# Value and output weights of a gated cross-attention layer multiplied in three rounded products

## The chip, the cores and the metric

The kernel runs on one core of one Trainium2 chip. The metric is the device time of one execution in microseconds (us). Three executions of the kernel before took 627.66, 628.72 and 630.34 us, the median being 628.72 us.

## The reference

A layer takes 1024 tokens of width 256 (16 sequences of 64) and a context of the same length and width 128. Cross-attention comes first, then self-attention and a mixture of experts:

```
q = rmsnorm(layernorm(x) @ Wq), k = rmsnorm(ctx @ Wk), v = ctx @ Wv      # 16 heads of 128
out = softmax(q k^T * scale) @ v ;  x = x + tanh(g_xattn) * (out @ Wo)
x = x + tanh(g_ffn) * (causal self-attention + experts of layernorm(x))
```

The kernel never forms v of the cross-attention. For each head it multiplies the value weights (128 x 128) by the output weights (128 x 256) once, `vo = Wv_h @ Wo_h`, and applies vo to the context rows that attention has averaged.

## The kernel before, in words

All work is written out by hand in one program per engine, in the fixed order in which each engine runs it, with semaphores between them. Stage a is the cross-attention, stage b the self-attention, stage m the experts. Each stage runs over two halves of 512 tokens. Stages a and b run over 8 pairs of heads per half, stage m over 25 chunks of hidden units.

Nearly every large product is made of "rounded products". An operand is rounded to float32r (`hi`), the rest is taken by subtraction (`lo`), and hi*hi + hi*lo + lo*hi replace one float32 product. VectorE makes most `hi` halves of weights by a copy (split_queries, L1491; split_values, L1517), ScalarE some of them, and GpSimd all `lo` halves through its helper `rest` (L1720).

The product vo is the exception. In the first half of stage a (`weighs_values`, 8 pairs), value_out (L692 to L699) multiplies the raw float32 weights of the two heads, `raw_a2`, straight into `bank_k`, 128 x 256 for each head. ScalarE rounds that result into `vo_hi` (take_value_out, L1117) and VectorE takes the rest `vo_lo` (split_value_out, L1526), which is the last thing in its body for a pair. The other pieces of the order that matter here:

- TensorE, pair u (cross_pair, L846): norm_q and scores of u, then context_values of the pair before (which writes bank_k among others and so waits for vo_lo of that pair), keys and queries of the next pair, the two outputs of the pair before, between them the second queries, and then value_out(u) and norm_k of the next pair (L718). project_keys for the next pair's first head waits for the semaphore `raw`: the VectorE product L1432 has read bank_s.
- VectorE, pair u (cross_pair, L1588): sums of squares (L1405 to L1409), scaling of the scores (L1432, L1437), maximum, lows of the context values (L1393), subtraction of the maximum (L1455), take_q (L1479), then in some pairs one piece in slot 2 of the preparation of the next tokens, then normalise (L1461 to L1465), the transposition L1473, the two copies L1491, and L1529. Pairs are counted from 0 here. Slot 2 holds the statistics of the second half's tokens (L1303 to L1309) in pair 3 and their mean subtraction `hn` (L1317, four instructions) in pair 4. Pair 5 turns the tokens.
- GpSimd, pair u (cross_pair, L1764): `wq_lo` and `wk_lo` of the two heads of the pair after the next (four subtractions), each after its `hi`. In pair 0 it also subtracts the second half of the context (`ctxt_lo`).
- SyncE: the weights raw_a2 of pair n are loaded again after value_out of pair n-1 (`vo_done`), and behind that in the same queue come the loads of the query and key weights of pair n+2.

Of the kernel before, what the change touches and what calls it, by code (L numbers as in the profile page):

```python
# [27 lines left out]
F32R = mybir.dt.float32r  # L28
# [4 lines left out]
P = 128  # L33
# [160 lines left out]
def flamingo_layer(nc, x, ctx_t, ctx, head_a, head_b, pair_v, chunk_m, small, out, shared_units):  # L194
    TOK, D = x.shape
    H = head_a.shape[0]
    C = ctx_t.shape[0]
# [19 lines left out]
    AQ, AK, AV, AO = 0, D, 0, C  # L217
# [14 lines left out]
    with ExitStack() as stack:  # L232
        def sb(name, shape, dt=F32):
            return stack.enter_context(nc.sbuf_tensor(name, shape, dt))
# [25 lines left out]

        raw_a = sb("raw_a", [P, 2 * A1])
        raw_a1 = [raw_a[:, p * A1:(p + 1) * A1] for p in range(2)]
        raw_a2 = [sb(f"raw_a2_{p}", [P, A2]) for p in range(2)]
        raw_b1 = [sb(f"raw_b1_{p}", [P, B1]) for p in range(2)]
        raw_b2 = [sb(f"raw_b2_{p}", [P, B2]) for p in range(2)]
        raw_m1 = [sb(f"raw_m1_{p}", [P, M1]) for p in range(2)]
# [64 lines left out]
        def stage_sems(tag, names):  # L331
# [1 line left out]
            return {n: sem(f"{tag}_{n}") for n in names.split()}  # L333

        A = stage_sems("a", "wq_hi wq_lo wk_hi wk_lo q_done k_done sq_q sq_k qt kt scores raw scaled max "
                       "sub exp sum inv norm attn_t vo_done vo_hi vo_lo ssk_done ssq_done ssq ln_q qt_1 "
                       "ln_k r_k r_q pv_done pv_hi pv_lo wo_done")

        B = stage_sems("b", "wq_hi wq_lo wk_hi wk_lo wv_hi wv_lo wo_hi wo_lo q_done k_done v_done qt kt vs scores scaled "
# [90 lines left out]
        def _(sp):  # L430
# [2 lines left out]
                sp.dma_start(raw_a1[h], head_a[2 * u.i + h, :, 0:A1]).then_inc(ld_a1[h], 16)  # L433

            def load_a2(u, h):
                sp.dma_start(raw_a2[h][:], head_a[2 * u.i + h, :, A1:A1 + A2]).then_inc(ld_a2[h], 16)

            def load_b1(u, h):
                sp.dma_start(raw_b1[h][:], head_b[2 * u.i + h, :, 0:B1]).then_inc(ld_b1[h], 16)
# [50 lines left out]
                load_m2(Unit(plan, "m", 0, h))  # L490
            for n in range(1, HALVES * PAIRS):
                if n < PAIRS:
                    sp.wait_ge(A["vo_done"], n)
                    for h in range(2):
                        load_a2(numbered("a", n), h)
                if n + 2 < HALVES * PAIRS:
                    reload_a1(n + 2)
# [58 lines left out]
        def _(pe):  # L556
# [135 lines left out]
            def value_out(u):  # L692

                pe.wait_ge(A["kt"], u.of(1) + 2)
                for h in range(2):
                    pe.wait_ge(ld_a2[h], 16 * u.n)
                    last = nc.tensor.matmul(bank_k[:, h * D:(h + 1) * D], raw_a2[h][:, AV:AV + C], raw_a2[h][:, AO:AO + D],  # L697
                                            start=True, stop=True)
                last.then_inc(A["vo_done"], 1)  # L699

            def norm_q(u):
# [568 lines left out]
        def _(v):  # L1270
# [248 lines left out]
            def split_out(u, h):  # L1519
# [3 lines left out]
                v.wait_ge(ld_b2[h], 16 * u.n)  # L1523
                nc.vector.tensor_copy(wo_hi[h][:], raw_b2[h][:]).then_inc(B["wo_hi"], 1)

            def split_value_out(u):  # L1526
                v.wait_ge(A["vo_hi"], u.n)
                two = slice(2 * u.i, 2 * u.i + 2)
                nc.vector.tensor_tensor(vo_lo[:, two, :], bank_k[:].rearrange("p (h n) -> p h n", h=2), vo_hi[:, two, :],  # L1529
                                        ALU.subtract).then_inc(A["vo_lo"], 1)  # L1530
# [57 lines left out]
            def cross_pair(u):  # L1588

                prev, nxt = u.prev(), u.next()  # L1590
                after = nxt.next()
                add_variance(u)
                scale_scores(u)
                hurried = prev and prev.very_first
                if hurried:
                    split_context_values(prev)
                take_max(u)
                if prev and not hurried:
                    split_context_values(prev)
                subtract_max(u)  # L1600
                if nxt.kind == "b":
                    split_values(nxt)
                    take_q(nxt, 0)
                if nxt.kind == "a":
                    take_q(nxt, 0)
                prepare_piece(*piece_at(u, 2), u)
                normalise(u)
                turn_weights(u)
                split_queries(after, 0, nxt)
                if after.kind == "b":  # L1610
                    split_keys(after, 0, nxt)
                prepare_piece(*piece_at(u), u)
                if nxt.kind == "b":
                    take_q(nxt, 1)
                split_queries(after, 1, nxt)
                if u.first and prev:
                    read_acc(prev)
                if not u.deferred:
                    split_context_values(u)
                if after.kind == "b":  # L1620
                    split_keys(after, 1, nxt)
                if u.weighs_values:
                    split_value_out(u)
# [93 lines left out]
        def _(pool):  # L1717
            def rest(lo, raw, hi, signal):

                nc.gpsimd.tensor_tensor(lo, raw, hi, ALU.subtract).then_inc(signal, 1)  # L1720
# [35 lines left out]
            def split_values(u):  # L1756
                pool.wait_ge(B["wv_hi"], u.n)
                rest(wv_lo[:], raw_v[:], wv_hi[:], B["wv_lo"])
# [5 lines left out]
            def cross_pair(u):  # L1764
                nxt = u.next()
                after = nxt.next()
                if nxt.kind == "b":
                    split_values(nxt)
                for h in range(2):
                    split_head(after, h)  # L1770
                if u.very_first:
                    pool.wait_ge(ctxt_hi_ready, HALVES)
                    rest(ctxt_lo[:, HT:TOK], ctxt[:, HT:TOK], ctxt_hi[:, HT:TOK], ctxt_lo_ready)
# [109 lines left out]
```

## Time and profile before

| what | value |
|---|---|
| median of 3 runs | 628.72 us |
| profiled execution, its own time | 627.96 us |
| span of the profiled execution | 626.1 us |
| TensorE matmuls | 617.8 us busy, 99% |
| VectorE | 461.7 us busy, 74% |
| ScalarE | 320.2 us busy, 51% |
| GpSimd | 254.0 us busy, 41% |
| mean granted TensorE clock | 1.00 |

The span runs from the first to the last instruction. A busy share is the time in which at least one instruction of an engine is under way; consecutive matmuls overlap in the record, so the distance from one start to the next is what one costs. In a row of the timeline the first number is the start in us and the second the length; "x4" means that four instructions are merged in it; the bracket tells how long the engine had been idle and what released it.

### The profile page before, as it was taken

To read this page: it belongs to the slowest core of one execution; us is meant where nothing else is said; L and a number is where in the kernel's file an instruction comes from. 1 tells how busy PE (TensorE), PEld (TensorE's weight loads), DVE (VectorE), ACT (ScalarE), POOL (GpSimd) and SP (SyncE) were. 2 spreads that over 40 slices of the span, in tenths; PEclk is the share of its full clock that TensorE was granted. 3 is DMA by queue.
4 is the path that set the end of the run, shared out by engine and by line. 5 is a ranking of instruction groups with operands and counts; after the bars stand their busy time and mean duration, and the time that the engine had idled before them with its cause. 6 is when DMAs were issued, how large, how long until landed. Compare 5 with 4: busy or idle time off the path is not lost.

```text
span 626.1 us, 17387 instructions
## 1 busy us (share of the span) xinstructions
PE 617.8 (99%) x6906; PEld 526.1 (84%) x6906; DVE 461.7 (74%) x934; ACT 320.2 (51%) x699; POOL 254.0 (41%) x336
## 2 busy tenths in 40 slices
PE   8999999999999999999999999999999999999997
PEld 6788888888889888999999889988878788888885
DVE  5979787997886886786677899567566976575554
ACT  6867677777743334243434333454476444444442
POOL 3221211313144334344343354345545665455552
PEclk9999999999999999999999999999999999999999
DMA  7532130111021322222231321123344333334442
GB/s 232 189 89 67 52 103 28 41 39 37 18 70 48 106 69 69 70 68 78 66 115 40 115 70 36 35 64 96 95 99 109 81 102 101 89 95 104 104 119 81
DMA packets 45757, 51.42 MB, mean 82 GB/s; under 512 B 12784, under 2 KB 32752, under 8 KB 45680
## 3 DMA queue, kind: packets, MB, share of 16 engines
q1 hardware_dynamic: 44976, 49.86, 27.8%
q8 instruction: 55, 0.90, 0.6%
q10 hardware_dynamic: 704, 0.48, 0.2%
q14 instruction: 22, 0.18, 0.1%
HBM read 48.22 MB, written 1.05 MB: 79 GB/s over the span
## 4 chain that ended last, share of the span: by engine, by line
PE 93%; ACT 3%; DVE 2%; issue 1%; DMA 1%; SPq 0%; DVEq 0%; ACTq 0%
PE bank_q L564 16%; PE acc L591 14%; PE bank_k L564 14%; PE acc L626 10%; PE bank_v L564 8%; PE bank_s L564 7%; PE bank_v L687 7%; PE bank_k L767 2%; PE bank_s L735 2%; PE bank_p L784 2%; PE bank_s L745 2%; PE bank_p L718 1%; PE bank_t L752 1%; PE bank_q L708 1%; PE bank_k L697 1%
## 5 line engine op out<-in xcount | busy, mean ns | idle before, releaser
L1720 POOL TENSOR_TENSOR wq_lo<-raw_a,wq_hi 128x256 fp32r<-128x256 f32 x32 | 23.5, 735 | 115.8 <-DVE wq_hi L1491 115.8
L1720 POOL TENSOR_TENSOR wq_lo<-raw_m,wq_hi 128x256 fp32r<-128x256 f32 x50 | 42.0, 840 | 60.9 <-DVE wq_hi L1510 59.5
L1554 DVE TENSOR_TENSOR pv_lo<-raw_a,pv_hi 128x512 fp32r<-128x512 f32 (+1 forms) x51 | 38.3, 753 | 30.8 <-ACT pv_hi L1135 30.2
L1135 ACT ACTIVATE pv_hi<-raw_a 128x512 fp32r<-128x512 f32 (+1 forms) x51 | 31.7, 623 | 55.4 <-DVE raw_a L1549 53.8
L564 PE MATMUL bank_q<-xt_hi,wq_hi 128*128 128x512 f32 x144 | 59.8, 416 | 0.0
L564 PE MATMUL bank_q<-xt_hi,wq_lo 128*128 128x512 f32 x144 | 56.8, 394 | 0.0
L564 PE MATMUL bank_q<-xt_lo,wq_hi 128*128 128x512 f32 x144 | 56.5, 393 | 0.0
L1541 DVE TENSOR_TENSOR r_k<-ln_k,unit_w 128x512 f32<-128x512 f32 x44 | 30.6, 696 | 32.1 <-ACT ln_k L1126 31.9
L1720 POOL TENSOR_TENSOR wk_lo<-raw_m,wk_hi 128x256 fp32r<-128x256 f32 x50 | 37.6, 753 | 30.5 <-ACT wk_hi L1210 30.5
L1720 POOL TENSOR_TENSOR wv_lo<-raw_v,wv_hi 128x512 fp32r<-128x512 f32 x16 | 20.7, 1294 | 67.9 <-DVE wv_hi L1517 67.9
L1720 POOL TENSOR_TENSOR wo_lo<-raw_m,wo_hi 128x256 fp32r<-128x256 f32 x50 | 41.5, 830 | 7.2 <-ACT wo_hi L1204 7.2
L1720 POOL TENSOR_TENSOR wq_lo<-raw_b,wq_hi 128x256 fp32r<-128x256 f32 x32 | 24.7, 772 | 48.5 <-DVE wq_hi L1494 48.5
L1057 ACT ACTIVATE kt<-bank_k 128x512 f32<-128x512 f32 x46 | 27.5, 599 | 32.2 <-PE bank_k L564 31.0
L564 PE MATMUL bank_k<-xt_hi,wk_lo 128*128 128x512 f32 x110 | 43.3, 394 | 0.0
L564 PE MATMUL bank_k<-xt_hi,wk_hi 128*128 128x512 f32 x110 | 43.2, 393 | 0.0
L564 PE MATMUL bank_k<-xt_lo,wk_hi 128*128 128x512 f32 x110 | 43.1, 392 | 0.0
L1069 ACT ACTIVATE vs<-bank_v 128x512 f32<-128x512 f32 x32 | 19.1, 598 | 44.6 <-PE bank_v L687 44.6
L626 PE MATMUL acc<-pv_hi,wo_hi 128*128 128x512 f32 (+1 forms) x102 | 40.6, 398 | 0.8 <-DVE pv_lo L1554 0.6
L626 PE MATMUL acc<-pv_hi,wo_lo 128*128 128x512 f32 (+1 forms) x102 | 40.1, 393 | 0.0
L626 PE MATMUL acc<-pv_lo,wo_hi 128*128 128x512 f32 (+1 forms) x102 | 39.9, 392 | 0.0
L591 PE MATMUL acc<-wo_hi,pv_hi 128*128 128x256 f32 x128 | 36.4, 284 | 0.0
L591 PE MATMUL acc<-wo_lo,pv_hi 128*128 128x256 f32 x128 | 36.2, 283 | 0.0
(254 smaller groups left out, 2097.3 us busy)
## 6 DMA issues: line engine op xcount, KB each, us to landing
raw_m<-in_chunk_m SPq DMA_DIRECT2D x50, 256.0 KB, 2.8
raw_a<-in_head_a SPq DMA_DIRECT2D x48, 192.0 KB, 3.1
raw_b<-in_head_b SPq DMA_DIRECT2D x32, 256.0 KB, 3.1
raw_m<-in_chunk_m SPq DMA_DIRECT2D x50, 128.0 KB, 2.1
raw_v<-in_pair_v SPq DMA_DIRECT2D x16, 256.0 KB, 2.9
raw_b<-in_head_b SPq DMA_DIRECT2D x32, 128.0 KB, 2.1
vs<-qt SPq DMA_DIRECT2D x32, 32.0 KB, 2.0
xs<-in_x SPq DMA_DIRECT2D x6, 128.0 KB, 3.3
```

The lines of the kernel that those rows point to most:

```text
L564: last = nc.tensor.matmul(bank[:], w[:, cols], m(k), start=n == 0, stop=n == 3 * chunks - 1)
L591: last = nc.tensor.matmul(acc[t // 2][:, (t % 2) * D:(t % 2 + 1) * D], w[:, tok], m, start=begins and n == 0, stop=True, skip_group_check= ...
L626: last = nc.tensor.matmul(acc[k][:, part], w[:, cols], m[:, part], start=u.first and n == 0, stop=True, skip_group_check=True)
L687: last = nc.tensor.matmul(bank_v[:, b * PAIR:(b + 1) * PAIR], m, w[:, cols], start=n == 0, stop=n == 3 * KD - 1)
L735: last = nc.tensor.matmul(bank_s[j * GROUP:(j + 1) * GROUP, g * SEQ:(g + 1) * SEQ], qt[:, h, queries], kt[:, h, at:at + SEQ], start=True, ...
L745: last = nc.tensor.matmul(bank_s[j * GROUP:(j + 1) * GROUP, g * SEQ:g * SEQ + seen], qt[:, h, queries], kt[:, h, at:at + seen], start=True ...
L1057: nc.scalar.activation(kt[:, h], bank[:], ACT.Copy).then_inc(stage["kt"], 1)
L1069: nc.scalar.activation(vs[u.n % 2][:, at:at + NT // 2, :], bank_v[:].rearrange("p (t n) -> p t n", n=PAIR), ACT.Copy).then_inc(B["vs"], 1)
L1135: nc.scalar.activation(pv_hi[:, u.parity, part], hh[:, part], ACT.Copy).then_inc(M["hh_hi"], 1)
L1541: nc.vector.tensor_tensor(gu, gs, weights, ALU.mult).then_inc(M["weighted"], 1)
L1554: nc.vector.tensor_tensor(pv_lo[:, u.parity, part], hh[:, part], pv_hi[:, u.parity, part], ALU.subtract)\
L1720: nc.gpsimd.tensor_tensor(lo, raw, hi, ALU.subtract).then_inc(signal, 1)
```

## The change

raw_a2 becomes one tensor for both heads of a pair (128 x 2 x 384). VectorE copies it, rounded, into `vo_in_hi` in one instruction after take_q and ahead of the piece in slot 2. GpSimd subtracts, in one instruction, into `vo_in_lo`, ahead of its four subtractions of the pair. value_out waits for vo_in_lo and issues three rounded products for each head in place of one float32 product. The load of the next raw_a2 waits for vo_in_lo in place of vo_done.

```diff
-        raw_a2 = [sb(f"raw_a2_{p}", [P, A2]) for p in range(2)]
+        raw_a2 = sb("raw_a2", [P, 2, A2])
+        vo_in_hi, vo_in_lo = sb("vo_in_hi", [P, 2, A2], F32R), sb("vo_in_lo", [P, 2, A2], F32R)
...
-                sp.dma_start(raw_a2[h][:], head_a[2 * u.i + h, :, A1:A1 + A2]).then_inc(ld_a2[h], 16)
+                sp.dma_start(raw_a2[:, h], head_a[2 * u.i + h, :, A1:A1 + A2]).then_inc(ld_a2[h], 16)
...
-                    sp.wait_ge(A["vo_done"], n)
+                    sp.wait_ge(A["vo_in_lo"], n)
...
                 pe.wait_ge(A["kt"], u.of(1) + 2)
+                pe.wait_ge(A["vo_in_lo"], u.n)
                 for h in range(2):
-                    pe.wait_ge(ld_a2[h], 16 * u.n)
-                    last = nc.tensor.matmul(bank_k[:, h * D:(h + 1) * D], raw_a2[h][:, AV:AV + C], raw_a2[h][:, AO:AO + D],
-                                            start=True, stop=True)
+                    for n, (w, m) in enumerate(((vo_in_hi, vo_in_hi), (vo_in_hi, vo_in_lo), (vo_in_lo, vo_in_hi))):
+                        last = nc.tensor.matmul(bank_k[:, h * D:(h + 1) * D], w[:, h, AV:AV + C], m[:, h, AO:AO + D],
+                                                start=n == 0, stop=n == 2)
...
+            def round_value_out(u):
+                for h in range(2):
+                    v.wait_ge(ld_a2[h], 16 * u.n)
+                if u.n > 1:
+                    v.wait_ge(A["vo_done"], u.n - 1)
+                nc.vector.tensor_copy(vo_in_hi[:], raw_a2[:]).then_inc(A["vo_in_hi"], 1)
...
                 if nxt.kind == "a":
                     take_q(nxt, 0)
+                if u.weighs_values:
+                    round_value_out(u)
                 prepare_piece(*piece_at(u, 2), u)
...
                     split_values(nxt)
+                if u.weighs_values:
+                    pool.wait_ge(A["vo_in_hi"], u.n)
+                    rest(vo_in_lo[:], raw_a2[:], vo_in_hi[:], A["vo_in_lo"])
                 for h in range(2):
                     split_head(after, h)
```

## Rows read from the trace of the kernel before

**Rows 1.** The page: busy time of TensorE, its granted clock in 40 slices, chain by engine

```profile
PE 617.8 (99%) x6906; PEld 526.1 (84%) x6906; DVE 461.7 (74%) x934; ACT 320.2 (51%) x699; POOL 254.0 (41%) x336
...
PEclk9999999999999999999999999999999999999999
...
PE 93%; ACT 3%; DVE 2%; issue 1%; DMA 1%; SPq 0%; DVEq 0%; ACTq 0%
```

**Rows 2.** Waits of TensorE in and after pair 0: us in total, times, longest

```profile
...
PE bank_p L718 <- ACT qt L1052: 0.8, 1, 0.8
...
```

**Rows 3.** The chain that ended last, pair 2: start, us, what

```profile
41.34 1.44 PE acc L591 x12
42.78 0.86 PE bank_k L697 x4
```

**Rows 4.** Timeline of VectorE, pair 2, with its start and end

```profile
38.64 0.68 DVE L1479 TENSOR_TENSOR qt<-bank_q,gqk 128x512 f32<-128x512 f32 x1
...
39.70 0.69 DVE L1461 TENSOR_REDUCE ex_sum<-ex 128x8 f32<-128x512 f32 x1 [0.38 <-ACT ex L1093]
...
40.66 0.69 DVE L1465 TENSOR_TENSOR attn<-ex,ex_inv 128x512 f32<-128x512 f32 x1
...
44.31 0.69 DVE L1529 TENSOR_TENSOR vo_lo<-bank_k,vo_hi 128x512 fp32r<-128x512 f32 x1 [1.76 <-ACT vo_hi L1119]
```

**Rows 5.** Groups by form: copies on VectorE, subtractions on GpSimd, 0 to 420 us

```profile
L1491 DVE CAST wq_hi<-raw_a 128x256 fp32r<-128x256 f32 x12 | 2.8, 267 | 0.0
...
L1517 DVE CAST wv_hi<-raw_v 128x512 fp32r<-128x512 f32 x16 | 6.7, 418 | 0.3 <-DMA raw_v<-in_pair_v 0.3
...
L1720 POOL TENSOR_TENSOR wq_lo<-raw_a,wq_hi 128x256 fp32r<-128x256 f32 x20 | 14.7, 737 | 66.3 <-DVE wq_hi L1491 66.3
```

**Rows 6.** Timelines of GpSimd and VectorE in a pair of stage b

```profile
206.75 1.29 POOL L1720 TENSOR_TENSOR wv_lo<-raw_v,wv_hi 128x512 fp32r<-128x512 f32 x1 [4.25 <-DVE wv_hi L1517]
...
207.53 1.05 DVE L1465 TENSOR_TENSOR attn<-ex,ex_inv 128x512 f32<-128x512 f32 x1
```

**Rows 7.** Timelines of VectorE and GpSimd at the start, 6.8 to 8.9 us

```profile
6.84 0.61 DVE L1317 TENSOR_SCALAR hn<-xs,mv 128x256 f32<-128x256 f32 x1
...
6.84 0.46 POOL L1720 TENSOR_TENSOR wk_lo<-raw_a,wk_hi 128x128 fp32r<-128x128 f32 x1 [5.38 <-ACT wk_hi L1234]
```

**Rows 8.** Timelines of VectorE and TensorE, pair 0

```profile
18.35 0.69 DVE L1479 TENSOR_TENSOR qt<-bank_q,gqk 128x512 f32<-128x512 f32 x1
...
19.56 1.02 PE L697 MATMUL bank_k<-raw_a 128*128 128x256 f32 x4
21.43 0.64 PE L718 MATMUL bank_p<-sq_k,ones_of 128*32 128x256 f32 x8 [0.84 <-ACT qt L1052]
```

**Rows 9.** Timelines of VectorE, GpSimd and the chain, pair 3

```profile
55.37 0.69 DVE L1529 TENSOR_TENSOR vo_lo<-bank_k,vo_hi 128x512 fp32r<-128x512 f32 x1 [0.29 <-ACT vo_hi L1119]
...
56.75 0.68 DVE L1432 TENSOR_TENSOR sc_sub<-bank_s,r_k 128x512 f32<-128x512 f32 x1
...
56.46 0.37 DVE L1409 TENSOR_TENSOR ssq<-sums_t,eps_q 128x8 f32<-128x8 f32 x1
...
56.08 0.73 POOL L1720 TENSOR_TENSOR wq_lo<-raw_a,wq_hi 128x256 fp32r<-128x256 f32 x1
...
57.70 0.90 PE bank_s L564 x3
```

**Rows 10.** Timeline of VectorE and the chain, pair 4

```profile
61.39 1.14 DVE L1317 TENSOR_SCALAR hn<-xs,mv 128x256 f32<-128x256 f32 x4
62.44 0.68 DVE L1461 TENSOR_REDUCE ex_sum<-ex 128x8 f32<-128x512 f32 x1
...
66.44 0.69 DVE L1529 TENSOR_TENSOR vo_lo<-bank_k,vo_hi 128x512 fp32r<-128x512 f32 x1 [1.17 <-ACT vo_hi L1119]
...
67.81 0.69 DVE L1432 TENSOR_TENSOR sc_sub<-bank_s,r_k 128x512 f32<-128x512 f32 x1
...
68.77 0.90 PE bank_s L564 x3
```

More of the change, by code:

```diff
@@ L335, in flamingo_layer @@
         A = stage_sems("a", "wq_hi wq_lo wk_hi wk_lo q_done k_done sq_q sq_k qt kt scores raw scaled max "
-                       "sub exp sum inv norm attn_t vo_done vo_hi vo_lo ssk_done ssq_done ssq ln_q qt_1 "
+                       "sub exp sum inv norm attn_t vo_in_hi vo_in_lo vo_done vo_hi vo_lo ssk_done ssq_done ssq ln_q qt_1 "
                        "ln_k r_k r_q pv_done pv_hi pv_lo wo_done")
```

## The prediction, made before the changed kernel had run

> **What bounds the kernel now.** I read the page first: matmuls are under way for 617.8 us of a span of 626.1, the chain that ended last is TensorE for 93%, and the granted clock is full, 2.4 GHz, in all 40 slices [rows 1]. So time is what TensorE issues plus what makes it wait. Next the waits of TensorE over the stretch that the change touches, the first half of stage a: from pair 0 on there is one, of 0.8 us, at norm_k in pair 0 [rows 2]. In pairs 1 to 7 TensorE runs without a gap, one pair every 11.07 us (the same step at 57.70 and 68.77 [rows 9, 10]), and every other engine has slack behind it. A saving on TensorE comes through in full there, and so does any new wait. The question is therefore what the products save, and whether the new VectorE copy and GpSimd subtraction use up the slack. All times below are read against the profiled execution, 627.96 us; it lies 0.76 below the median of 628.72.
>
> **The products.** In the chain, value_out of a pair takes 0.86 us (four records, two for each float32 product), and the twelve rounded products of the same 128x128 by 128x256 shape ahead of it take 1.44, 0.12 each [rows 3]. Six of them cost 0.72. The saving is 0.14 us a pair, where nothing else is late; over eight pairs at most 1.1 us. Bounds: nothing saved (0.86 again, should the six not follow each other so closely), or 0.2 a pair.
>
> **The copy on VectorE.** 128x768 has no row. 128x256 takes 0.27 and 128x512 0.42 [rows 5], so 0.15 for each 256, and 0.57 for 768; the low end is 0.5, the high end three separate 128x256, 0.8. I take 0.58.
>
> **The subtraction on GpSimd.** 128x256 takes 0.74 [rows 5], 128x512 1.29 [rows 6]: 0.55 for each 256, 1.85 for 768. Ends: 1.7, and 2.2 for three of 0.74.
>
> **What the long subtraction does to VectorE.** This is the larger cost. In stage b a GpSimd subtraction runs from 206.75 to 208.04; the VectorE product attn (ex times ex_inv, both in SBUF) begins at 207.53 and takes 1.05 us [rows 6] where it takes 0.69 otherwise [rows 4]. It ends 0.54 after the subtraction does, so it stood until GpSimd was through. The Trainium skill states it (SBUF — State Buffer, "Who interferes with whom"): an instruction of VectorE with two SBUF inputs, or a copy or scalar operation in its two-port mode, and one of GpSimd exclude each other for the whole instruction; tensor_reduce never contends. By that page and by these rows the sum is the same, but it speaks against this change, so it is worked through pair by pair.
>
> **Pairs 1, 2, 5, 6, 7.** Pair 2 stands for them [rows 4]. take_q begins at 38.64 and the next instruction can begin 0.6 later: copy 39.24 to 39.82. The sum over ex, which waits for ScalarE until about 39.7 anyway, shifts by 0.1. GpSimd, which has been idle for microseconds, subtracts from 39.9 to 41.75. attn wants to begin at 40.8, ends at 42.3 instead of 41.35: VectorE is now 0.95 late. It stays late until vo_lo, before which it had 1.76 us of idle time [rows 4]. So 0.8 is left, and the pair's end is as before. TensorE wants vo_in_lo as the second output ends, by the chain at 42.78 [rows 3], and has it at 41.8. No wait, 0.14 gained: 5 x 0.14 = 0.7 us. In pair 5 the cover is thinner, as two subtractions for the turned tokens lie behind attn.
>
> **Pair 0.** Here take_q begins at 18.35 [rows 8]: copy 18.95 to 19.53, GpSimd 19.6 to 21.45. TensorE, with no outputs to do, wanted to begin value_out at 19.56 and now begins at 21.5. It ends at 22.2, and norm_k begins then instead of 21.43 [rows 8]; the old 0.8 us wait there, for ScalarE's qt, hides the rest. ScalarE's vo_hi and what follows it (a context split, ln_k) move by 0.9 too, level with TensorE. Cost 0.8 us, bounds 0.6 and 1.2 (with the ends of copy and subtraction).
>
> **Pair 3.** Only 0.29 us of idle time lie before vo_lo, as the statistics fill VectorE [rows 9]. Copy 0.58 and a bit for the lock make it 0.6 late there, 0.3 after the idle time. The next thing that TensorE waits for is sc_sub, which ended at 57.43 with TensorE there by the chain at 57.70 [rows 9]: a slack of 0.27 at most; I use 0.2. So TensorE is 0.1 late, its 0.14 included. But ssq, two inputs, already stood behind a GpSimd subtraction here (0.37 us; the one from 56.08 to 56.81 [rows 9]), and with everything shifted it can meet the next one from its start: 0.4 more. I take 0.3; bounds 0.1 and 0.6.
>
> **Pair 4.** The four hn follow the copy at once, and they contend with GpSimd: at the start one of them took 0.61 where four in a row take 1.14 [rows 10], while GpSimd's subtraction, begun within the series, took its usual 0.46 [rows 7]. So a waiting GpSimd instruction gets in between two hn, and the next hn stands until it is through. Here: copy to 61.97, first hn, GpSimd from 62.2 to 64.05, then three hn, and the sum over ex begins at 64.8, not 62.44: 2.4 late [rows 10]. 1.17 of that goes into the idle time before vo_lo, 0.2 into the slack between sc_sub's end (68.50) and TensorE (68.77) [rows 10]. 1.0 us comes through, 1.5 if ssq stands behind a GpSimd subtraction again. I take 1.2. If all four hn went first, it would be 0.
>
> **Loads.** The next raw_a2 is asked for up to 0.8 us earlier than before, and is needed some 3 us earlier, at the copy; a period is 11 us, so at nothing. In pair 0 it is asked for 0.9 later, with 6 us to go. The four GpSimd subtractions and the reloads behind them in the SyncE queue move by 1 us within the same 11 us: nothing.
>
> **Sum.** 0.8 + 0.3 + 1.2 - 0.7 = +1.6 us (bounds of the parts: 0 to +2.9): 629.6 for an execution like the profiled one, 630.3 as a median. What TensorE loses in stage a it doesn't regain, for it has no gap later.
>
> **The rivals.**
> - *Only the saving shows* (the four hn go first, ssq slips by): pair 3 and pair 4 at zero, five or six pairs gain 0.14, pair 0 costs 0.8 or less. -0.1 to -0.5, 628.4. For it: the long idle times of VectorE before vo_lo [rows 4, 10]. Against: rows 7. Chance 0.2.
> - *No cheaper products*: the six rounded products take as long as the float32 ones, and the change doesn't do what it says. The 0.7 falls away: +2.3, 631.0. Rows 3 speak against it. Chance 0.08.
> - *Slower by over 0.5%*: GpSimd's 768 columns in one instruction take more than the row's slope gives. Place: each pair's attn and vo_in_lo. The point from which it decides: 2.6 us in place of 1.85; then attn eats the last 0.8 of VectorE's idle time in the plain pairs, and vo_in_lo comes after TensorE wants it. At 3 us each of the seven later pairs loses 0.4 to 0.5 and pairs 0 and 4 another 1.2 each: 1.6 + 0.7 + 3.2 + 2.4, about +7, 635.6; at 2.6 about +4, 632.7. For it: a subtraction of 128x256 and one of 128x512 are all there is. Against: their durations hardly vary. Chance 0.12.
>
> **How the numbers follow.** The forecast has the remaining 0.6. The likeliest time is 630.3. The range goes from 627.8, for the second case and an execution at the lower end of the runs shown, to 632.6, where the last case begins; a tenth is left out above, less than that below. About 0.5%, 3.1 us, is what a measurement of this kernel can tell from no change. Faster by that much would need three times the whole saving: 0.02. Slower by that much is the last case and the upper corner of the forecast: 0.13. The same: 0.85.
>
> **What would show it.** In the chain, value_out at 0.72 us for six products. On VectorE, one copy of 128x768 at 0.58; on GpSimd, one subtraction at 1.85; attn at 1.5 to 1.7 us in the plain pairs. TensorE's waits: pair 0, value_out for vo_in_lo, 1.9 us, with the 0.8 at norm_k gone; pair 4, about 1 us, at the context values for vo_lo or at project_keys for sc_sub; pair 3, a few tenths. An idle time before vo_lo of 0.8 us left in the plain pairs. I am wrong if TensorE waits in a plain pair, if one hn of pair 4 isn't lengthened by some 1.8 us, or if value_out takes as long as before.

## The result, and the profile after

| | before | after |
|---|---|---|
| median (9 executions each, same chip) | 628.77 us | 632.36 us |
| lowest to highest | 627.66 to 630.34 | 630.48 to 633.77 |
| profiled execution, its own time | 627.96 us | 633.46 us |
| span | 626.1 us | 631.7 us |

The ratio is 1.0055, with an interval of 1.0044 to 1.0065: the change costs 3.6 us. The predicted range (627.8 to 632.6) holds that, the predicted 630.3 does not reach it, and 0.55% is just past the 0.5% that separated "the same" from "slower". So the sign was right and the size was less than half of what came. The sections below say where the other 2 us are. The executions of one kernel spread over 2 to 3 us, and the profiled ones are single executions: that of the kernel before lies 0.8 us under its median, that of the changed kernel 1.1 us above.

The page of the changed kernel; [rows 1] answer to its first, third and last line:

```profile
PE 619.3 (98%) x6922; PEld 528.5 (84%) x6922; DVE 474.1 (75%) x942; ACT 320.5 (51%) x699; POOL 268.3 (42%) x344
...
PEclk9899999999999999999999999999999999999999
...
PE 88%; DVE 6%; ACT 3%; issue 2%; DMA 1%; POOL 0%; SPq 0%; DVEq 0%; ACTq 0%
```

TensorE is still the chain for 88% of the span, but VectorE now has 6% in place of 2%, and the second slice of the granted clock shows an 8 where before there was none. The waits of TensorE from 17 to 420 us (us in total, times, longest) answer to [rows 2]:

```profile
PE bank_k L699 <- POOL vo_in_lo L1731: 1.8, 1, 1.8
PE bank_t L786 <- issue: 1.0, 2, 0.6
PE bank_s L565 <- DVE sc_sub L1434: 1.0, 2, 0.5
PE bank_p L720 <- ACT qt L1054: 1.0, 1, 1.0
PE bank_p L786 <- issue: 0.8, 1, 0.8
PE bank_k L769 <- issue: 0.6, 1, 0.6
```

Three are forecast: 1.8 us in pair 0 at value_out, and sc_sub twice (pairs 3 and 4). "issue" at L769 is the forecast wait of pair 4 under another name: that product of context_values begins at 71.16, and vo_lo ended at 71.05. The wait on qt lies in the second half and was there before. The other two issue lines (three waits, 1.8 us) are in stage b, which the change doesn't touch; before, the whole run had this one such line:

```profile
PE bank_t L784 <- issue: 0.2, 1, 0.2
```

The two new operations, by their tile (lowest, mean and highest ns):

```profile
L1533 DVE CAST vo_in_hi<-raw_a x8: 550/551/553, 19.2 to 99.4; 128x768 fp32r<-128x768 f32 x8
L1731 POOL TENSOR_TENSOR vo_in_lo<-raw_a,vo_in_hi x8: 1807/1850/1886, 19.8 to 100.0; 128x768 fp32r<-128x768 f32 x8
```

The chain that ended last, pairs 0, 2 and 4:

```profile
19.84 1.82 POOL vo_in_lo L1731
21.79 0.95 PE bank_k L699 x6
...
24.10 1.71 PE bank_s L737 x64
...
34.55 0.72 PE bank_k L699 x6
...
65.06 2.64 DVE hn L1319 x4
```

And the timeline of VectorE, pairs 2 to 4, which answers to [rows 4, 9, 10]:

```profile
43.44 1.61 DVE L1467 TENSOR_TENSOR attn<-ex,ex_inv 128x512 f32<-128x512 f32 x1
...
46.86 0.69 DVE L1538 TENSOR_TENSOR vo_lo<-bank_k,vo_hi 128x512 fp32r<-128x512 f32 x1 [0.62 <-ACT vo_hi L1121]
...
59.20 0.75 DVE L1411 TENSOR_TENSOR ssq<-sums_t,eps_q 128x8 f32<-128x8 f32 x1
...
64.98 2.73 DVE L1319 TENSOR_SCALAR hn<-xs,mv 128x256 f32<-128x256 f32 x4
```

attn stands behind the subtraction on GpSimd (0.69 before), four hn take 2.73 us (1.14 before), and of the 1.76 us that VectorE was idle before vo_lo 0.62 are left.

To see where the time went, I cut each profiled execution at the same products. A pair runs from the first key product after one context_values to the same product of the next pair (column k is the time between those of pair k and k+1; the first holds value_out of pair 0). "Half 2" is the second half of stage a, from the last such mark to the first output product of stage b; "b" is stage b to its last output product. The last column is the length of TensorE's program against the kernel before, in instructions, as TensorE's records count it (matmuls, weight loads, waits and a few others: 14,240 in the kernel before; of e2's one is missing).

| us | 0 | 1 | 2 | 3 | 4 | 5 | 6 | 7 | half 2 | b | span | program |
|---|---|---|---|---|---|---|---|---|---|---|---|---|
| before | 6.93 | 11.06 | 11.08 | 11.06 | 11.07 | 11.94 | 11.08 | 11.24 | 103.9 | 206.1 | 626.1 | 0 |
| after | 9.52 | 10.93 | 10.93 | 11.49 | 12.22 | 11.86 | 10.93 | 11.10 | 103.7 | 208.4 | 631.7 | +32 |
| e1 | 7.98 | 11.32 | 10.99 | 11.49 | 12.23 | 11.89 | 10.94 | 11.09 | 103.6 | 207.2 | 628.6 | +32 |
| e2 | 8.04 | 11.32 | 11.01 | 11.47 | 12.23 | 11.87 | 10.94 | 11.10 | 103.7 | 208.7 | 630.7 | +47 |
| e3 | 7.20 | 11.33 | 10.99 | 11.49 | 12.23 | 11.90 | 10.91 | 11.11 | 103.7 | 208.4 | 629.9 | +28 |
| e4 | 7.21 | 11.32 | 11.00 | 11.09 | 11.07 | 11.81 | 10.93 | 11.09 | 103.9 | 206.7 | 627.2 | +20 |
| e5 | 7.20 | 11.21 | 11.09 | 11.09 | 11.08 | 11.94 | 11.09 | 11.24 | 104.0 | 207.8 | 628.3 | +32 |
| e6 | 7.98 | 11.31 | 10.97 | 11.51 | 12.22 | 11.88 | 10.93 | 11.09 | 103.7 | 207.1 | 628.5 | +256 |
| e7 | 9.67 | 11.08 | 11.07 | 11.40 | 12.23 | – | – | 11.24 | 103.7 | 205.9 | 629.3 | 0 |
| e8 | 7.20 | 11.08 | 10.93 | 10.93 | 10.98 | 11.82 | 10.95 | 11.10 | 103.9 | 208.6 | 628.4 | +40 |
| e9 | 8.09 | 11.38 | 11.00 | 12.35 | 11.64 | 11.89 | 10.94 | 11.10 | 103.7 | 207.3 | 629.4 | +32 |
| e10 | 7.99 | 11.32 | 11.00 | 11.49 | 11.56 | 11.89 | 10.93 | 11.10 | 103.7 | 207.0 | 628.2 | +32 |
| e11 | 9.62 | 11.06 | 11.08 | 11.05 | 11.09 | 11.96 | 11.07 | 11.23 | 103.9 | 207.5 | 629.3 | +4 |
| e12 | 7.21 | 11.22 | 11.07 | 11.09 | 11.07 | 11.96 | 11.07 | 11.37 | 105.2 | 207.1 | 628.9 | +256 |

(A dash: the marking record is missing from the trace.) The eight pairs of the changed kernel cost 3.5 us more than before, and stage b 2.3. Pair 0 alone has 2.6 of the 3.5, where 0.8 was forecast. Its rows say why: after its wait TensorE issues 64 scores in 1.71 us (0.89 in every other pair), and the granted clock in steps of one us (us; PE busy, count; clock; DMA share; GB/s) has fallen to half:

```profile
22.00:23.00 1.00, 1.00 (x14) 1.00 0.99 332
23.00:24.00 1.00, 1.00 (x24) 0.63 1.03 361
24.00:25.00 1.00, 1.00 (x48) 0.50 0.56 200
25.00:26.00 1.00, 1.00 (x36) 0.50 0.56 133
26.00:27.00 1.00, 1.00 (x28) 0.66 0.64 154
27.00:28.00 1.00, 1.00 (x15) 1.00 0.39 137
```

So TensorE, idle for 1.83 us until 21.79, ran at 1.2 in place of 2.4 GHz in the steps from 24 to 26 and in parts of those at either end: by the means of 0.63 and 0.66, from 23.3 to 26.7. Before, all six steps are at 1.00. That and stage b became the questions.

### The profile page after: what moved, and what is told of

The parts are those of the page before. It is cut to its first block, busy times and chain, and to the rows that moved or that the text cites. A ratio compares the mean times of both kernels' runs of the same rounds, so it can differ in the third digit from the quotient of the medians.

```text
span 631.7 us, 17443 instructions
## 1 busy us (share of the span) xinstructions
PE 619.3 (98%) x6922; PEld 528.5 (84%) x6922; DVE 474.1 (75%) x942; ACT 320.5 (51%) x699; POOL 268.3 (42%) x344
## 3 DMA queue, kind: packets, MB, share of 16 engines
HBM read 48.22 MB, written 1.05 MB: 78 GB/s over the span
## 4 chain that ended last, share of the span: by engine, by line
PE 88%; DVE 6%; ACT 3%; issue 2%; DMA 1%; POOL 0%; SPq 0%; DVEq 0%; ACTq 0%
PE bank_q L565 16%; PE acc L592 13%; PE bank_k L565 13%; PE acc L627 10%; PE bank_v L565 7%; PE bank_v L688 7%; PE bank_s L565 7%; PE bank_p L786 2%; PE bank_s L747 2%; PE bank_k L769 2%; PE bank_s L737 2%; PE bank_t L754 1%; PE bank_q L710 1%; PE bank_p L720 1%; DMA xt<-in_ctx_t 1%
## 5 line engine op out<-in xcount | busy, mean ns | idle before, releaser
L592 PE MATMUL acc<-vo_hi,pv_hi 128*128 128x256 f32 x128 | 36.2, 283 | 0.0
```

Of the source, the lines that this page charges most:

```text
L592: last = nc.tensor.matmul(acc[t // 2][:, (t % 2) * D:(t % 2 + 1) * D], w[:, tok], m, start=begins and n == 0, stop=True, skip_group_check= ...
```

## The experiments

Every kernel ran in turn with the kernel before on one chip; ratios are to that. The kernel before had medians of 628.47 (e1 to e4), 628.43 (e5 to e8), 628.54 (e9 to e11) and 629.52 us (e12).

**e1, the changed kernel again**, unedited: is the fall of the clock there each time?

> The changed kernel once more, beside the others on one chip. Both theories: 1.003 to 1.007 of the kernel before. What it is to show is the granted clock in pair 0: the theory that TensorE's 1.8 us wait in pair 0 costs a second time through the clock expects a stretch of about 3 us at 1.2 GHz within 22 to 28 us again, where the kernel before has none.

631.36 us, 1.0044 (1.003 to 1.0058). The profiled execution has the same waits, but 1.00 in every step of pair 0, and that pair takes 7.98 us in place of 9.52, so the fall costs it 1.54 us. Pair 1 gives 0.39 of that back (10.93 with the fall, 11.32 without), which leaves 1.15. Each execution also lists its mean granted clock. Over the six kernels that have the 1.8 us wait (after, e1, e6, e7, e10, e11) it is 0.997 or less in 24 of 48 executions; over those without it (e2 to e5, e8, e9, e12, with 0.9 us of wait in e9) in none of 66, and in none of the 82 of the kernel before that ran beside e1 to e12. Executions with the low clock are longer by 2.0 us in after (633.2 against 631.2), 1.7 in e6, 1.4 in e10 and in e11, 1.0 in e7, and not longer in e1 (two of five). So the wait lets the clock fall about every second time, and by the two traces that is some 0.6 us in the mean.

**e2, the wait filled**: eight products of zeros, ahead of value_out in pair 0, write bank_k, which value_out overwrites.

```diff
+                if u.very_first:
+                    for _ in range(8):
+                        nc.tensor.matmul(bank_k[:], zeros[:, 0:P], zeros[:], start=True, stop=True)
```

> The changed kernel, with 8 products of zeros (some 1.85 us) into bank_k ahead of the wait for vo_in_lo in pair 0, so that TensorE has something to do; the products are overwritten and the output is the same. Theory A (the clock falls because TensorE stood still, and the slow stretch costs about 1.6 us): granted clock 1.00 throughout, value_out at the same moment as without the filling or 0.2 us later, time 1.5 us under the changed kernel where that shows the slow stretch. Theory B (the clock fell for another reason, or the fall costs nothing because the other engines set the pace there): same time as the changed kernel within 0.3 us.

631.66 us, 1.0045 (1.0032 to 1.0059). The clock fell in none of its five executions, as expected, but the median is no lower than that of e1. Pair 0 takes 8.04 us, so the filler costs next to nothing there; in the profiled execution stage b, at 208.7, has 2.2 us of issue waits and took the gain. On the median this run settles nothing.

**e3, float32 in pair 0 alone**: the wait is taken away by computing value_out of pair 0 as before, without copy and subtraction.

```diff
+                if u.i in (0,):
+                    for h in range(2):
+                        pe.wait_ge(ld_a2[h], 16 * u.n)
+                        last = nc.tensor.matmul(bank_k[:, h * D:(h + 1) * D], raw_a2[:, h, AV:AV + C],
+                                                raw_a2[:, h, AO:AO + D], start=True, stop=True)
...
-                if u.weighs_values:
+                if u.weighs_values and u.i not in (0,):
                     round_value_out(u)
```

> The changed kernel with the float32 product in pair 0 alone, without its copy, subtraction and wait. Theory A (pair 0 costs its wait, 0.8 us net, and the slow clock after it, 1.6 us): 2.4 us under the changed kernel, so +1.0 to +1.3 us against the kernel before, all of it from pairs 3 and 4 less the saving of the others. Theory B (pair 0 costs only its wait): 0.8 us under the changed kernel.

630.25 us, 1.0028 (1.0017 to 1.0038): 1.1 us below e1 (the intervals overlap), 1.8 above the kernel before where 1.0 to 1.3 was expected, no fall of the clock. Pair 0 is at 7.20, though, not at 6.93, and pair 1 keeps the 11.33 of e1. VectorE and GpSimd of this kernel at that place:

```profile
23.56 0.75 DVE L1424 TENSOR_TENSOR ssq<-sums_t,eps_q 128x8 f32<-128x8 f32 x1
...
25.01 1.48 DVE L1452 TENSOR_TENSOR sc<-sc_sub,r_q 128x512 f32<-128x512 f32 x1
...
23.56 0.72 POOL L1744 TENSOR_TENSOR wq_lo<-raw_a,wq_hi 128x256 fp32r<-128x256 f32 x1
...
24.66 1.29 POOL L1744 TENSOR_TENSOR ctxt_lo<-xt,ctxt_hi 128x512 fp32r<-128x512 f32 x1
```

And the same four in the kernel before:

```profile
23.30 0.17 DVE L1409 TENSOR_TENSOR ssq<-sums_t,eps_q 128x8 f32<-128x8 f32 x1
...
24.32 0.71 DVE L1437 TENSOR_TENSOR sc<-sc_sub,r_q 128x512 f32<-128x512 f32 x1
...
23.30 0.76 POOL L1720 TENSOR_TENSOR wq_lo<-raw_a,wq_hi 128x256 fp32r<-128x256 f32 x1
...
24.44 1.74 POOL L1720 TENSOR_TENSOR ctxt_lo<-xt,ctxt_hi 128x512 fp32r<-128x512 f32 x1
```

In both, ssq of VectorE and wq_lo of GpSimd are recorded from the same moment. Before, ssq went first (0.17 us), and later ctxt_lo stood behind sc (1.74). In e3 GpSimd went first: ssq stood for 0.6 us, sc for 0.8. I call that a race. What decides it isn't in the record: the instructions just ahead of the two (vo_lo and the first wq_lo) begin 0.03 us apart before as in e3. It falls this way also in e4 and e8, and in e5 and e12, where pairs 0 and 1 compute as before: 7.20 and 11.2 us. Of these six traces VectorE wins it in the one of the kernel before alone, so 6.93 and 11.06 may be the rarer outcome for that kernel; e5 and e12 are the fairer measure for pairs 0 and 1.

**e4, float32 in pairs 0, 3 and 4**: the same edit with `(0, 3, 4)`, so that only the pairs stay rounded in which the forecast had a gain.

> The changed kernel with the float32 product in pairs 0, 3 and 4, and rounded products in pairs 1, 2, 5, 6 and 7. The theory of the prediction (the plain pairs hide copy, subtraction and the exclusion of the two engines, and gain 0.14 us each; the whole loss lies in pairs 0, 3 and 4): 0.5 to 0.7 us faster than the kernel before. The rival (the work on VectorE and GpSimd costs something in every pair): not faster than the kernel before.

629.54 us, 1.0016 (1.0007 to 1.0025). Pairs 3 and 4 are back at 11.09 and 11.07, pairs 5 to 7 keep their gain of 0.13 to 0.15, and still the kernel is 1 us slower than before, where 0.5 to 0.7 us faster was expected. What is left: 0.28 in pair 0 and 0.26 in pair 1 (the race of e3), and 0.6 us in stage b.

**e5, the kernel before with a longer program**: 64 more waits on TensorE, for a count reached long ago, in 32 places of the first projections. The compiled program has 32 instructions more, as many as the change adds.

```diff
+                        if pad[0] > 0:
+                            for _ in range(2):
+                                pe.wait_ge(setup_pool, SETUP)
+                            pad[0] -= 1
                         last = nc.tensor.matmul(bank[:], w[:, cols], m(k), start=n == 0, stop=n == 3 * chunks - 1)
```

> The kernel before, with waits on a semaphore that has long been set put between the products of the first pairs of stage a. Its TensorE program has 32 instructions more, as many as the changed kernel's, and does nothing else. Theory S (stream: in stage b TensorE now and then stands because its next instructions have not been loaded, and 32 instructions of shift put the places where it does so into the runs of small products of head_values): stage b, from the first acc<-wo_hi product to the last, 207.2 to 208.7 us instead of 206.1, idle times put down to issue at head_values (L784 in the kernel before) of 1 to 2 us in all, time 1.0 to 2.3 us over the kernel before. Theory T (those idle times come from what the change does to VectorE and GpSimd, or are chance): stage b 206.1, time within 0.4 us of the kernel before.

629.65 us, 1.0015 (1.0006 to 1.0024): slower by itself. Pairs 2 to 7 are as before, stage b is at 207.8 (206.1 before), and TensorE's waits between 17 and 420 us now have:

```profile
PE bank_t L791 <- issue: 0.8, 2, 0.5
PE bank_p L791 <- issue: 0.5, 1, 0.5
```

They sit at the 64x64 products of head_values, whose starts lie some 0.02 us apart in the record. So a longer program is enough to slow the kernel, with the computation and the data unchanged, and in the trace most of the loss is in stage b. Pair 0 and pair 1 show the race of e3 here (7.20 and 11.21, 0.42 us together), so part of the 0.15% may be that.

The traces tell more of these waits. I counted TensorE's records from the first on. In all 14 traces there are 34 issue waits of over 0.1 us apart from eight at context_values that end 0.1 us after vo_lo, and all 34 end at number 193 or 194 of a block of 256 records, whatever the kernel; the eight stand elsewhere in a block. At each of the 34 a packet of the queue `q8 instruction` had begun 2.2 to 2.9 us before TensorE went on, and the last 256 records had taken 2.0 to 5.8 us without the wait, where a whole pair of stage a takes 11 us. So the waits stand where TensorE crosses from one load of instructions to the next soon after the last crossing. What the longer program changes is the product at the crossing. Record 8386 falls on a long product (128x512) in the kernel before, e7 and e11, and shows no wait; in the nine traces of programs 20 to 47 instructions longer it falls among the 64x64 products, and all nine have a wait there, for 0.2 to 0.9 us.

**e6, the changed kernel with 224 more**, so that the program is 256 instructions longer than before. The page of the changed kernel gives 0.90 MB of instructions in 55 packets, so 16 KB each; with TensorE's 14,272 records that is about 260 records a packet. If only the place within such a packet counted, 256 would put stage b back.

```diff
+            PAD[0] = 224
```

> The changed kernel, with 224 such instructions more in stage a, so that its TensorE program is 256 longer than that of the kernel before when stage b begins; the loads of instructions are 16 KB each in the trace, which is 256 of 64 bytes. Theory S: stage b back to 206.1 to 206.5 us, issue idle times at head_values under 0.5 us, time 1 to 2 us under the changed kernel, if the 224 waits themselves are hidden behind the products. Theory T: stage b stays at 207.2 to 208.7.

630.31 us, 1.0032 (1.0019 to 1.0045), 1.0 us below e1 (the intervals overlap). Stage b is at 207.1 with 1.0 us of issue waits, where 206.1 to 206.5 was expected: as e1 has it (207.2), so the profile shows no return to the old value. The clock fell in 3 of 8 executions.

**e7, the copies alone**: copy and subtraction are made and waited for, but the float32 product is kept. TensorE's program has exactly the old length.

```diff
-                    for n, (w, m) in enumerate(((vo_in_hi, vo_in_hi), (vo_in_hi, vo_in_lo), (vo_in_lo, vo_in_hi))):
-                        last = nc.tensor.matmul(bank_k[:, h * D:(h + 1) * D], w[:, h, AV:AV + C], m[:, h, AO:AO + D],
-                                                start=n == 0, stop=n == 2)
+                    last = nc.tensor.matmul(bank_k[:, h * D:(h + 1) * D], raw_a2[:, h, AV:AV + C], raw_a2[:, h, AO:AO + D],
+                                            start=True, stop=True)
```

> The changed kernel with its copies, subtractions and waits, but with the float32 products in value_out again (and the next load waits for them too). Theory of the prediction with theory S: pairs 2, 5, 6 and 7 take 11.07, 11.94, 11.08 and 11.24 us as in the kernel before, pairs 0, 1, 3 and 4 lose 1.2, 0.3, 0.4 and 1.2; the TensorE program has the length of before, so stage b takes 206.1: 2.7 to 3.2 us over the kernel before. Theory T: stage b takes 207.2 or more, 4 us over the kernel before.

631.09 us, 1.0038 (1.0025 to 1.0051). The plain pairs are at 11.08 and 11.07: the copy and the subtraction cost nothing there, and all of the 0.14 comes from the products. Stage b is at 205.9 with a single issue wait of 0.2. The clock fell in this execution too:

```profile
22.00:23.00 1.00, 1.00 (x12) 0.99 0.94 339
23.00:24.00 1.00, 1.00 (x16) 0.50 0.45 99
24.00:25.00 1.00, 1.00 (x37) 0.50 0.89 301
25.00:26.00 1.00, 1.00 (x44) 0.50 0.70 173
26.00:27.00 1.00, 1.00 (x35) 0.80 0.69 171
```

**e8, the products alone**: six rounded products, but of constants; the split of the weights is left out, and vo is computed from them, which is what its time is to be read as.

```diff
-                if u.weighs_values:
-                    round_value_out(u)
...
+            nc.gpsimd.memset(vo_in_hi[:].bitcast(F32), 0.5).then_inc(A["vo_in_hi"], 1)
+            nc.gpsimd.memset(vo_in_lo[:].bitcast(F32), 0.0).then_inc(A["vo_in_lo"], 1)
```

> The changed kernel with its rounded products in all eight pairs, but without the copies, subtractions and their waits: the products read constants written once at the start, so the split of the weights is left out. The prediction's own term: each pair 0.14 us shorter than in the kernel before, except pair 0, where TensorE waits for qt anyway: 1.0 us off stage a. Theory S adds 1 to 2.5 us in stage b (32 instructions more), so 0 to 1.5 us over the kernel before in all; theory T: 1.0 us under the kernel before.

629.34 us, 1.0009 (1.0001 to 1.0018). Pairs 2 and 3 are at 10.93, 0.15 and 0.13 less than before, with no split to pay for. Against e5, which has the same outcome of the race, the eight pairs take 0.95 us less, the forecast 1.0. The kernel isn't faster all the same: stage b is at 208.6, with

```profile
PE bank_t L789 <- issue: 1.5, 2, 1.1
PE bank_p L789 <- issue: 0.6, 1, 0.6
```

**e9, the subtraction on VectorE**, right behind the copy, so that no GpSimd instruction stands in the way of attn and hn.

```diff
+                v.wait_ge(A["vo_in_hi"], u.n)
+                nc.vector.tensor_tensor(vo_in_lo[:], raw_a2[:], vo_in_hi[:], ALU.subtract).then_inc(A["vo_in_lo"], 1)
```

> The changed kernel with the subtraction into vo_in_lo made by VectorE, right behind its copy, in place of GpSimd. Theory L (what costs in pairs 0 and 4 is the long subtraction on GpSimd: TensorE waits for it, attn and hn stand behind it): attn back to 0.69 us, the four hn back to 1.14, VectorE's extra work 0.55 + 1.0 = 1.6 us a pair; vo_in_lo is there 0.8 us sooner in pair 0, so pair 0 loses about 0.3 instead of 1.05 and TensorE's wait there drops to 1.0 us, with no fall of the clock; pair 4 loses about 0.3 instead of 1.16; pair 3 loses about 1.0 instead of 0.4, since its VectorE has no idle time. Pairs 2, 5, 6, 7 as in the changed kernel. In all 1 us under the changed kernel. Theory M (only the amount of added VectorE time matters, and the exclusion is a side show): VectorE's own extra time is more than in the changed kernel, and pairs 3 and 4 both get longer, by 0.5 us or more.

631.56 us, 1.0043 (1.0027 to 1.006): no gain in all, but each pair tells something. VectorE in pair 4:

```profile
64.91 0.96 DVE L1535 TENSOR_TENSOR vo_in_lo<-raw_a,vo_in_hi 128x768 fp32r<-128x768 f32 x1
65.78 1.14 DVE L1319 TENSOR_SCALAR hn<-xs,mv 128x256 f32<-128x256 f32 x4
```

hn is back at 1.14 and attn at 0.69; pair 4 falls from 12.23 to 11.64. Pair 3, where VectorE is full [rows 9], pays for its 0.96 us: 12.35 in place of 11.49. The wait of pair 0 is halved to 0.9 us, and the clock fell in none of nine executions; but pair 0 takes 8.09, where the theory had 7.2. The waits of TensorE from 17 to 30 us say why:

```profile
PE bank_k L699 <- DVE vo_in_lo L1535: 0.9, 1, 0.9
PE bank_s L565 <- DVE sc_sub L1434: 0.5, 1, 0.5
PE bank_k L769 <- issue: 0.4, 1, 0.4
```

With 1.5 us of copy and subtraction VectorE has no idle time left in pair 0 and is late for vo_lo (23.21 to 23.90, in e3 from 22.48), then for sc_sub: two new waits of 0.9 us together in place of the one shortened.

**e10, hn ahead of the copy in pair 4**:

```diff
-                if u.weighs_values:
+                if u.weighs_values and u.i != 4:
                     round_value_out(u)
                 prepare_piece(*piece_at(u, 2), u)
+                if u.weighs_values and u.i == 4:
+                    round_value_out(u)
```

> The changed kernel with the four hn of pair 4 ahead of the copy; nothing else moved. Theory L (a waiting GpSimd subtraction gets in between two hn and holds up the rest): hn back to 1.14 us from 2.73, attn of pair 4 lengthened instead by about 1 us, vo_in_lo there at about the moment that TensorE wants it; pair 4 takes 11.2 to 11.6 us instead of 12.23. Theory M (pair 4 is long because copy, hn and the rest are simply too much work): 12.2 us again.

631.42 us, 1.0041 (1.0027 to 1.0056). In pair 4:

```profile
63.59 1.13 DVE L1319 TENSOR_SCALAR hn<-xs,mv 128x256 f32<-128x256 f32 x4
64.64 0.55 DVE L1533 CAST vo_in_hi<-raw_a 128x768 fp32r<-128x768 f32 x1
```

The pair falls to 11.56, by 0.67, from the order of two pieces alone; attn now stands behind the subtraction (1.60 us), as expected. The lock between VectorE and GpSimd is therefore what lengthened hn. The median doesn't show it: the clock fell in 6 of 10 executions, 2 of 5 in e1.

**e11, rounded products in pair 0 alone**: the edit of e3 with the pairs 1 to 7. The program is 4 instructions longer than before.

> The kernel before with the change made in pair 0 alone (copy, subtraction, wait and rounded products), the float32 product in pairs 1 to 7. 4 instructions more on TensorE. Theory of the clock: pair 0 takes 7.98 us instead of 6.93 where the clock holds and 9.5 where it falls to 1.2 GHz after the wait, which it does in some two of five executions, seen as a mean granted clock of 0.997 or less; those are 1 to 2 us longer than the others. In all 1.0 to 2.5 us over the kernel before, the later pairs and stage b within 0.3 us of it. Rival (the fall of the clock is not tied to this wait): no execution at 0.997 or less, or as many among those of the kernel before.

631.34 us, 1.0033 (1.0019 to 1.0047), the clock low in 5 of 10 executions, and stage b at 207.5 with 1.3 us of issue waits. Pairs 1 to 7 are as before to 0.02. The median is 2.8 us above the kernel before, past the 1.0 to 2.5 expected, and stage b is 1.4 above, where 0.3 was expected. One pair of eight makes most of the loss: 1.1 us for the wait, 1.5 in every second execution for the clock (together the 9.62), and stage b.

**e12, the kernel before with 256 more**: e5 with 256 in place of 32, and the clean counterpart to e6.

> The kernel before with 256 wait instructions on TensorE, each for a count that was reached long ago, spread over the key projections of the first head pairs; nothing of the computation changes. Rivals on the issue waits of stage b (before: 0.2 us and 206.1 us; with 32 such instructions 1.3 us and 207.8 us). Theory S' (only the position of the stage's instructions relative to loads of 256 instructions counts): 256 more put stage b where it was, so 206.1 to 206.4 us for the stage, issue waits of 0.3 us or less, and a median within 0.4 us of the kernel before. Theory S'' (the position matters, but not by 256): stage b 206.6 us or more, and a median 0.4 to 1.6 us above before. If the waits themselves cost TensorE time in stage a, the plain pairs show it: 11.07 us before; more than 11.10 means they do.

629.41 us, 1.0004 (0.9993 to 1.0015). The median is that of the kernel before, as with the first theory; the profiled execution goes with the second: stage b is at 207.1, half 2 1.2 us longer than before (0.8 of it two issue waits, at 135.3 and 205.8, both at crossings as in e5), and

```profile
PE bank_p L791 <- issue: 0.7, 2, 0.5
PE bank_v L774 <- issue: 0.6, 1, 0.6
PE bank_t L791 <- issue: 0.5, 1, 0.5
```

Its span, 628.9, is 2.8 above that of before where the medians differ by 0.1, so this execution is no typical one. What the run does show: the number of instructions isn't the price, since eight times the padding of e5 cost no more on the median, and the plain pairs, at 11.07, aren't touched by it.

No version ran faster than the kernel before.

## Why the prediction came near, and what it left out

Where both clocks are full, e1 is the execution to set beside the forecast. That the stated range held the 632.36 is in part luck: its top, 632.6, was set by a rival, a slower GpSimd, that did not come about, and what filled it, the clock and stage b, had no term in the sum.

| term | forecast | e1 | |
|---|---|---|---|
| pair 0 | +0.8 (0.6 to 1.2) | +1.05 (+0.78 against e5) | within its bounds |
| pair 1 | -0.14 | +0.26 (+0.11 against e5) | the failed step |
| pairs 2, 5, 6, 7 | -0.14 each | -0.09, -0.05, -0.14, -0.15 | |
| pair 3 | +0.3 (0.1 to 0.6) | +0.43 | |
| pair 4 | +1.2 | +1.16 | |
| half 2 | 0 | -0.30 | |
| stage b | not considered | +1.1 (after: +2.3) | missing |
| clock in pair 0 | not considered | 0 (after: +1.5) | missing |

**The products.** Six cost 0.72 us, the pair gains 0.14; e7 and e8 show that the whole gain comes from them. In pairs 2 and 5, 0.05 and 0.09 of it are missing in e1.

**Copy and subtraction.** 0.55 (forecast 0.58) and 1.85 us (forecast 1.85). The slope between the two sizes that the trace had was enough; the rival of a GpSimd too slow fell. Its price was mis-added: 1.6 + 0.7 + 3.2 + 2.4 is 7.9, not about 7. So was that of the rival "only the saving shows": with pair 0 at its own bounds of 0.6 to 0.8 it gives +0.1 to -0.2, not -0.1 to -0.5. Neither decided anything.

**The lock between the two engines.** It was the largest term and was right in kind and in size. attn took 1.61, as forecast; the 0.8 us of idle time forecast before vo_lo was 0.62; ssq of pair 3 stood for 0.75 as suspected; four hn took 2.73. GpSimd did get in between two hn, which the one pair of [rows 7] had to carry, and e10 shows it by turning the order round, e9 by taking GpSimd out. The Trainium skill (SBUF — State Buffer, "Who interferes with whom") has the exclusion and says that the instruction issued first gets the shared ports while the other blocks. These rows agree: in pair 4 the subtraction begins at 65.14 and the second hn at 65.24, and that hn takes 1.94 us (0.35 before).

**The plain pairs.** "Pair 2 stands for them" was the step that failed, for pair 1: at its start GpSimd still has the four subtractions and ctxt_lo of pair 0, and ssq and sc of VectorE run into them if they lose the race that e3 shows. In e1 sc took 1.48 us (0.71 before), and of the 1.75 us of idle time before the vo_lo of pair 1 there is 0.01 left, where the forecast counted on 0.8. That is 0.4 us in e1 against the forecast; 0.15 of it is in e5 and e12 too, so it comes from the race without the change. Nor do all of these pairs take 11.07: in the kernel before pair 5 takes 11.94 and pair 7 11.24. In the first trace of the changed kernel, where the slow clock had held TensorE back, pair 1 was at 10.93.

**Pair 0.** That a new wait on TensorE comes through in full left out that it may cost more than itself, since an idle TensorE may come back slower. The forecast named the wait of 1.9 us (it was 1.8) and priced it by the trace of before, in which after the start TensorE waits for 0.8 us at most [rows 2] and never with a fall of the clock. No row there bounded it. e9's 0.9 us did not bring it on in nine executions, 1.8 us did in 24 of 48.

**Stage b.** The sum held the edited stage alone. e5 shows that 32 idle instructions cost the kernel 0.15%, in its trace mostly in stage b, and e7, with copy, subtraction and the old program length, keeps stage b at 205.9. Together: the spans of e1 and after lie 2.5 and 5.6 us above that of before, the latter 4.4 without its fall of the clock; with 0.6 for the clock in the mean that gives 3.1 and 5.0, and the median says 3.6. In that, stage m and the end took 0.8 us less in e1 than before (212.3 against 213.1), which they do in e7 and e11 too, and I can't say why.

**What stays open.** How much of the 3.6 us stage b has in the mean. The two kernels of the old length have 206.1 and 205.9, all others 206.7 to 208.7, at +4 as at +256; but these are single executions, and after and e1, the same program, differ by 1.2. The crossings explain where TensorE waits, not how long: number 7106 cost 0.15 us in the kernel before, 0.65 in after, nothing over 0.1 in e1. That instructions came late there is argued from the places and the packets: no run changed the loads alone. Nor was it shown what decides, at the same wait, whether the clock falls.

## What to carry to other kernels

Before work is handed to GpSimd, lay its whole instruction over what VectorE does beside it: once it is under way, every operation with two inputs in SBUF that it meets waits for its end (attn, ssq and sc here; sc_sub, which reads a bank of PSUM, kept its 0.68 us), and in a row of short ones GpSimd gets in between. The order of two pieces was worth 0.7 us of the 1.2 here. And a saving of 0.14 us a pair is smaller than what a longer instruction stream or one new wait on a TensorE that had none can cost; for gains of that size, test by padding the old kernel to the new length (e5) and by one changed pair alone (e11).

## What the runs showed that I had not expected

- The clock falls from 2.4 to 1.2 GHz in about half of the executions with the same 1.8 us of idle time, and costs 1.54 us in pair 0, of which pair 1 gives 0.39 back. It doesn't fall during the idle time but after TensorE has taken up work again: 1.5 us after in the changed kernel (21.79 and 23.3), some 0.4 us after in e11 (21.57; the step from 22 is at 0.51), and in each of the three traces that have it it is back after 3.4 us.
- TensorE can wait for its own instructions in a straight program. The page of the changed kernel shows the loads:

```profile
q8 instruction: 55, 0.90, 0.6%
```

  The Trainium skill (Runtime: NRT & Kernel Launch, "Instruction fetch mechanics") has a program streamed in blocks of 16 KiB, the cost of crossing a boundary "mostly hidden". The packets have that size here, and all 34 issue waits stand at one place of a block of 256 records. Most crossings show no wait, but up to 2.3 us in one stage (e8) were not hidden.
- Where VectorE and GpSimd ask at the same recorded moment, either can go first: ssq took 0.17 us in one trace and 0.75 in another at the same place of the program.
